# A mixer's transform split into 121 by 25, and its second norm turned by fp8 products

## The reference, cut to what matters

```python
x = conv(x)                      # x: (64, 55, 55, 96); depthwise 25x25, every third tap; gate, bias, residual
t = x.reshape(64, 3025, 96)      # 55 * 55 = 3025 tokens = 25 * 121
# mixer
h = relu(bn1(layernorm(t) @ w1.T))                    # 96 -> 192 channels
X = fft(h, axis=1, norm='ortho')                      # along the 3025 tokens
xr = relu(X.real * diag(r) - X.imag * diag(i) + rb)
xi = relu(X.imag * diag(r) + X.real * diag(i) + ib)
y = ifft(xr + 1j * xi, axis=1, norm='ortho').real
t = t + bn2(y @ w2.T)                                 # 192 -> 96
# feed-forward: inputs and weights of each product rounded to 5 exponent and 2 mantissa bits
n = q8(layernorm(t))
a = relu(q16(q16(n @ q8(W1).T) + q8(b1)))             # 96 -> 384
t = t + q16(q16(q8(a) @ q8(W2).T) + q8(b2))           # 384 -> 96
```

## Time and profile before

| | |
|---|---|
| median of 3 runs | 6499.09 us (6497.29 to 6509.12) |
| the profiled execution | 6508.48 us |
| its span | 6506.7 us |
| mean granted TensorE clock | 0.923 |
| TensorE busy | 5635.0 us (87%) |
| VectorE busy | 4653.9 us (72%) |
| ScalarE busy | 3317.6 us (51%) |
| GpSimd busy | 2185.0 us (34%) |

### The profile page before, as it was taken

How to read it: one execution, slowest core, us unless ns; L and a number is a source line. 1 busy time by engine, 2 the same in 40 slices (tenths; PEclk the granted TensorE clock), 3 DMA queues, 4 the chain that set the end, 5 groups by cost and what they waited for, 6 DMA issues and landing times. The chain is left out here.

```text
span 6506.7 us, 139542 instructions
## 1 busy us (share of the span) xinstructions
PE 5635.0 (87%) x43722; PEld 4751.2 (73%) x43722; DVE 4653.9 (72%) x13238; ACT 3317.6 (51%) x6661; POOL 2185.0 (34%) x1924
## 2 busy tenths in 40 slices
PE   8899994698888888888888888888888888888886
PEld 8898994577777777777777777777777777777775
DVE  4555664367777777777777777777777777777776
ACT  0000000356666666666666666666666666666664
POOL 0000000134444444444444444444444444444443
PEclk9999997789999999999999999999999999999996
DMA  6666664455555555555555555555555555555552
GB/s 219 181 179 189 178 184 113 101 128 132 128 129 129 129 129 128 128 127 128 127 128 128 128 128 128 128 128 128 128 129 129 129 129 128 128 129 129 129 127 60
DMA packets 877318, 875.70 MB, mean 135 GB/s; under 512 B 433439, under 2 KB 805535, under 8 KB 868895
## 3 DMA queue, kind: packets, MB, share of 16 engines
q1 hardware_dynamic: 806005, 784.39, 48.8%
q10 hardware_dynamic: 71174, 89.35, 4.5%
HBM read 497.81 MB, written 375.77 MB: 134 GB/s over the span
## 5 line engine op out<-in xcount | busy, mean ns | idle before, releaser
L646 POOL TENSOR_TENSOR spec<-spec,gc 96x385 f32<-96x385 f32 x512 | 485.7, 949 | 2506.6 <-DVE spec L837 2506.6
L655 POOL TENSOR_TENSOR z<-z,b2q 110x384 f16<-110x384 f16 x448 | 558.7, 1247 | 1622.7 <-ACT z L753 1622.7
L978 PEld LDWEIGHTS ps<-fb,acol 110*96 110x96 f32 (+1 forms) x7168 | 737.9, 164 | 358.9 <-DVE gv L841 230.6
L978 PE MATMUL ps<-fb,acol 110*96 110x110 f32 (+1 forms) x7168 | 817.9, 264 | 122.3 <-DVE gv L841 110.7
L686 ACT ACTIVATE hid<-ps,rstd 110x192 f32<-110x192 f32 x1792 | 660.0, 427 | 487.8 <-PE ps L948 487.2
L958 PE MATMUL ps<-hid,fa 110*110 110x384 f32 x1792 | 754.8, 503 | 165.7 <-ACT hid L686 83.0
L1005 PE MATMUL ps<-w2t,spec 97*110 97x96 f32 x3584 | 742.6, 293 | 13.7 <-DVE spec L848 6.2
L948 PE MATMUL ps<-w1t,xnt 97*110 97x192 f32 x3584 | 734.1, 327 | 0.6 <-ACT xnt L678 0.6
L245 DVE SCALAR_TENSOR_TENSOR xout<-cps,xin 114x351 f32<-114x351 f32 (+3 forms) x512 | 402.4, 786 | 443.4 <-PE cps L272 443.4
L1007 PE MATMUL ps<-w2t,spec 96*110 96x96 f32 x3584 | 718.4, 286 | 0.0
L827 DVE COPY arow<-ps 110x384 f32<-110x384 f32 x896 | 494.6, 552 | 288.0 <-PE ps L958 218.1
(11 more groups left out here) (103 smaller groups left out, 11789.9 us busy)
## 6 DMA issues: line engine op xcount, KB each, us to landing
a_d<-arow SPq DMA_DIRECT2D x896, 165.0 KB
acol<-a_d SPq DMA_DIRECT2D x64, 1155.0 KB
acol<-a_d SPq DMA_DIRECT2D x64, 1113.8 KB
out<-o_sb SPq DMA_DIRECT2D x832, 82.5 KB
xin<-in_x SPq DMA_DIRECT2D x256, 211.5 KB, 5.4
g_d<-mixed SPq DMA_DIRECT2D x64, 660.0 KB
x_d<-xout ACTq DMA_DIRECT2D x144, 263.2 KB
tok<-x_d SPq DMA_DIRECT2D x64, 577.5 KB
```

The source lines that it names most:

```text
L655: nc.gpsimd.tensor_tensor(z16[c % 2][:, :, :], z16[c % 2][:, :, :], b2, ALU.add).then_inc(z_biased, 1)
L978: last = nc.tensor.matmul(ps[0:HH, 2 - 2 * (t % 2) + n // 4, 128 * (n % 4):128 * (n % 4) + NP], acol[0:kk, k1, hf * HH:(hf + 1) * HH], fb[ ...
```

## The change

The transform is split into 121 by 25. A token is u (121) and s (25), 3025 without padding. A tile has 121 partitions and 25 columns; chunks have 4, 4, 4, 4, 3, 3, 3 columns (`CHUNK`), the last three second halves have one. The first half of the transform is over u; of 121 frequencies 61 are kept (`KH`), and two of them share a product with 25 columns each, real and imaginary: 100 partitions (`Q`), 31 pairs (`PAIRS_K`) in place of 28 frequencies. `rows` writes 128 partitions (`M`). The gates' tiles have 8, 8, 8, 7 pairs of 50 elements (400 and 350), `mix` and `inverse` go by 5, 5, 5, 4, 4, 4, 4 pairs (`MIXED`). Tokens, spectra and output need one transfer where two stood. The fills of `tok`, `t_res` and `grow` with zeros go.

Apart from that `xn2` becomes fp8, written so by VectorE, and it is turned by a plain product with an fp8 identity in place of a transpose by the f32 one.

```diff
-K1 = R // 2 + 1
-J = 28
-NP = 2 * R
+U = 121
+S = 25
+N = U * S
+KH = U // 2 + 1
+PAIRS_K = (KH + 1) // 2
+SLOTS = PAIRS_K + 1
+M = 4 * SLOTS
+Q = 4 * S
+CHUNK = (0, 4, 8, 12, 16, 19, 22, 25)
+MIXED = (0, 5, 10, 15, 19, 23, 27, 31)
+GROUP = (0, 8, 16, 24, 31)
+PART = (0, 7, 13, 19, 25)
...
+        ident8 = sb("ident8", [U, U], F8)
...
-        xn2 = sb("xn2", [NP, J, C])
+        xn2 = sb("xn2", [U, S, C], F8)
...
-                nc.vector.memset(tok[:, :, 0:C], 0.0)
-                for v in (t_res, grow):
-                    nc.vector.memset(v[:, :, :], 0.0)
+                nc.vector.memset(mixed[:, PAIRS_K, :], 0.0)
+                nc.vector.tensor_copy(ident8[:, :], ident[0:U, 0:U], saturate=False)
...
-                        for pp in range(2):
-                            sp.dma_start(a_d[i, :, pp * J + JC * c:pp * J + JC * (c + 1), :],
-                                         arow[c % AR][pp * R:(pp + 1) * R, :, :]).then_inc(a_stored[c % AR], 16)
+                        c0, c1 = CHUNK[c], CHUNK[c + 1]
+                        sp.dma_start(a_d[i, c0:c1, :, :].rearrange("s m h -> m s h"),
+                                     arow[c % AR][:, 0:c1 - c0, :]).then_inc(a_stored[c % AR], 16)
...
-                    for ri in range(2):
-                        src = a_d[i, ri * K1:ri * K1 + K1 - ri, 0:R, :].rearrange("k n h -> n k h")
-                        sp.dma_start(acol[ri * R:(ri + 1) * R, ri:K1, :], src).then_inc(acol_in, 16)
+                    src = a_d[i].rearrange("s (r p) h -> (s r) p h", p=SLOTS)
+                    for p0, p1 in ((0, 16), (16, PAIRS_K)):
+                        sp.dma_start(acol[:, p0:p1, :], src[:, p0:p1, :]).then_inc(acol_in, 16)
...
-                    for j in range(JC * c, JC * (c + 1)):
+                    for j in range(CHUNK[c], CHUNK[c + 1]):
                         last = nc.vector.tensor_scalar(xn2[:, j, :], t2[:, j, :], mean2[1][:, j:j + 1],
-                                                       rstd[1][:, j:j + 1], ALU.subtract, ALU.mult)
+                                                       rstd[1][:, j:j + 1], ALU.subtract, ALU.mult, saturate=False)
...
-                    nc.tensor.matmul(ps[0:NP, 7, 0:2 * H], fa[:, :],
-                                     hid[h % 2][:, :, :].rearrange("p j h -> p (j h)"),
+                    n = half(h)[1] - half(h)[0]
+                    nc.tensor.matmul(ps[0:M, 7, 0:n * H], fa[:, :],
+                                     hid[h % 2][:, 0:n, :].rearrange("p j h -> p (j h)"),
...
-                    for n in range(JC):
-                        k1 = c * JC + n
-                        o = ps[0:NP, c % 2, n * C:(n + 1) * C]
-                        nc.tensor.matmul(o, spec[0:HH + 1, 0, k1, :], w2t[0:HH + 1, 0, :],
+                    for p in range(MIXED[c], MIXED[c + 1]):
+                        n = p - MIXED[c]
+                        o = ps[0:Q, c % 2, n * C:(n + 1) * C]
+                        nc.tensor.matmul(o, spec[0:HH + 1, 0, p, :], w2t[0:HH + 1, 0, :],
...
-                        for j in range(JC):
-                            last = nc.tensor.transpose(ps[0:C, 4 + c % 2, 128 * j:128 * j + NP],
-                                                       xn2[:, JC * c + j, :], ident[0:NP, 0:NP])
+                        pe.sem_inc(pe_passed, 1)
+                        for j in range(CHUNK[c + 1] - CHUNK[c]):
+                            last = nc.tensor.matmul(ps[0:C, 4 + c % 2, 128 * j:128 * j + U],
+                                                    xn2[:, CHUNK[c] + j, :], ident8[:, :], start=True, stop=True)
```

More of the change, by code:

```diff
@@ L110, with half @@
 ROOT_C = 3
-QJ = J // 4
-PAIRS = NC * 2
 TILE_AT = (0, 2, 4, 6, 7, 9, 10, 12)
-TOK = JC * NP
+def half(h):
+    c0, c1 = CHUNK[h // 2], CHUNK[h // 2 + 1]
+    return (c0, c0 + 2) if h % 2 == 0 else (c0 + 2, c1)
 def transform_constants():
[L119 to L130, removed]
-    co, si = np.cos(th) / R, np.sin(th) / R
[L132 to L144, removed]
@@ L313, in mixer_stage @@
[L313 to L317, removed]
-        xn2 = sb("xn2", [NP, J, C])
-        xq = sb("xq", [C, J * NP], F8)
+        b2q = sb("b2q", [U, C], F16)
+        tok = sb("tok", [U, S, C + 1])
+        xnt = [sb(f"xnt{s}", [C + 1, JC, U]) for s in range(2)]
+        hid = [sb(f"hid{s}", [U, 2, H]) for s in range(2)]
+        arow = [sb(f"arow{s}", [M, JC, H]) for s in range(AR)]
@@ new lines, in mixer_stage @@
+        acol = sb("acol", [Q, PAIRS_K, H])
+        spec = sb("spec", [HH + 1, 2, PAIRS_K, Q])
+        gc = [sb(f"gc{s}", [HH, KC, Q // 2]) for s in range(2)]
+        gq = [sb(f"gq{s}", [HH, KC, Q // 2]) for s in range(2)]
+        gv = [sb(f"gv{s}", [HH, KC, Q // 2]) for s in range(2)]
+        mixed = sb("mixed", [Q, SLOTS, C])
+        grow = sb("grow", [M, S, C])
+        t_res = sb("t_res", [U, S, C])
+        t2 = sb("t2", [U, S, C])
+        xn2 = sb("xn2", [U, S, C], F8)
+        xq = sb("xq", [C, N], F8)
@@ L331, in mixer_stage @@
+        rstd = [sb(f"rstd{s}", [U, S]) for s in range(2)]
         ps = ctx.enter_context(nc.psum_tensor("ps", [128, 8, 512], F32))
@@ L688, in relu @@
+                    act.wait_ge(a_done, i * HALVES + max(h - 1, 0))
+                    s0, s1 = half(h)
+                    for j in range(s1 - s0):
+                        last = nc.scalar.activation(hid[h % 2][:, j, :], ps[0:U, 5 + h % 2, j * H:(j + 1) * H],
+                                                    ACT.Relu, scale=rstd[0][:, s0 + j:s0 + j + 1])
                     last.then_inc(hid_ready, 1)
                 def gate_in(t):
[L691 removed]
+                    p0, p1, _, hf = group(t)
@@ L709, in part @@
                     turn_out(0)
-                for h in range(PAIRS + 2):
-                    if first and 1 <= h <= PAIRS:
+                for h in range(HALVES + 2):
+                    if first and 1 <= h <= HALVES:
                         relu(h - 1)
@@ L863, in residual_stats @@
                     dve.wait_ge(t2_ready, (i - 2) * NC + c + 1)
-                    return stats(t2, 1, JC * c, JC * (c + 1))
+                    return stats(t2, 1, CHUNK[c], CHUNK[c + 1])
                 if second:
                     dve.wait_ge(w2_done, (i - 1) * NC)
-                for h in range(PAIRS + 3):
-                    if first and 2 <= h < PAIRS + 2:
+                for h in range(HALVES + 3):
+                    if first and 2 <= h < HALVES + 2:
                         rows_out(h - 2)
```

305 lines of the change are left out of this document (164 added, 141 removed).

## The result

| | before | changed |
|---|---|---|
| median | 6498.19 us (4 runs) | 6906.34 us (4 runs, 6899.69 to 6923.9) |
| ratio | | 1.0635 (95%: 1.0609 to 1.0661) |
| span of the profiled execution | 6506.7 us | 6899.0 us |
| mean granted TensorE clock | 0.923 | 0.823 |
| one iteration of the mixer's loop | 81.93 us | 88.74 us |

A forecast was written before the change was run, and what follows sets the result against it. VectorE was taken to bound stage A, TensorE and its clock much of stage C; -3.8 us gave 74.5 at full clock, a fall 78.5; 59 x 3.4 plus ends, -232, gave about 6270 us, range 6020 to 6440.

The forecast's parts named there:

- The work at full clock: One iteration of the mixer's loop without a clock fall: 78.3 us less 3.8, so 74.5 us.
- stage A: First 33.1 us (turns, first products, spectra), bounded by VectorE: fewer copies and norm operations, -1.2 us.
- stage B: Next 6.8 us, where the second norm is turned: shorter turns and evictions, `mix(0)` +0.2; sum -0.4 us.
- stage C, first part: `up(0)` to the second `down`: wider `mix`, `inverse` and `up`, partly covered by less idle time; +0.3 us.
- middle: Chunk steps of stage C with TensorE full: 4.27, 3.94, 3.78, 3.30 us for 4.17 three times and 3.57; -0.8.
- end: Fourth inverse row product to the next first copy, VectorE's and GpSimd's chain: fewer elements and statistics, -1.7 us.
- The clock: One fall an iteration, earlier, in stage B, priced at 3.6 to 5.1 us, taken as 4.0: 78.5 us.
- Slower: Rival, chance 0.10: clock falls in stage B, low until mid stage C (25 us); 84.0 us an iteration, about 6590 us.
- The first rival: Chance 0.17: no clock fall in the steady part; 74.5 us an iteration, about 6025 us.
- Transfers: Loads and stores of spectra, `acol` and `tok`: bytes same within 5%, other run lengths, waits stay hidden.
- The ends: Setup fills -8.4 us, first `acol` wait -5, shorter first and last iterations -16; about -30, bounds 15 and 45.

The follow-up runs named there:

- after_fill: The changed kernel with ten idle products (128x128 f32, into a bank nothing reads) in TensorE's waits of stage B; 6150.81 us, ratio 0.9451.
- before_fill: The kernel before with seven idle products (128x128 f32) ahead of the second `down`; 6295.95 us, ratio 0.9676.
- after_rows128: The changed kernel with `mix` and `up` on 128 rows of the array, the added rows holding zeros; 6261.22 us, ratio 0.9618.
- split_only: The changed kernel with the second norm in f32 and its turn by f32 transposes again, 121 by 25 kept; 6177.81 us, ratio 0.9488.
- best: The changed kernel with `mix` and `up` on 128 rows, six idle products in stage B and eight ahead of the last `down`; 6098.11 us, ratio 0.9366.
- after_fill32: The changed kernel with ten idle products in stage B standing on 32 rows of the array, not 128; 6444.73 us, ratio 0.9899.

## Why the prediction was wrong, by its own steps

**The work at full clock** came out within 0.3 us of the sum in each part but the last. TensorE's rows at the edges of the stages, of the iteration of before without a fall and then of after_fill (first `rows`, last `rows`, `up(0)`, second `down`, fourth `inverse_rows`, first `rows` of the next):

```profile
1443.11 0.85 PE L958 MATMUL ps<-hid,fa 110*110 110x384 f32 x2
...
1477.18 0.90 PE L958 MATMUL ps<-hid,fa 110*110 110x384 f32 x2 [1.32 <-ACT hid L686]
...
1484.64 0.72 PE L1048 MATMUL ps<-xq,w1q 96*128 96x440 fp8e5 x3 [0.80 <-ACT xq L726]
...
1494.10 0.78 PE L1064 MATMUL ps<-w2q,hq 128*110 128x96 fp8e5 x12 [1.81 <-issue]
...
1510.90 0.82 PE L928 MATMUL ps<-grow,ia 110*110 110x384 f32 x2
...
1520.94 0.85 PE L958 MATMUL ps<-hid,fa 110*110 110x384 f32 x2
```
```profile
3010.59 0.83 PE L992 MATMUL ps<-hid,fa 121*128 121x384 f32 x2
...
3043.57 0.59 PE L992 MATMUL ps<-hid,fa 121*128 121x192 f32 x2
...
3050.68 0.77 PE L1092 MATMUL ps<-xq,w1q 96*128 96x484 fp8e5 x3 [0.74 <-ACT xq L750]
...
3060.20 0.84 PE L1108 MATMUL ps<-w2q,hq 128*121 128x96 fp8e5 x12 [1.15 <-issue]
...
3076.30 0.83 PE L961 MATMUL ps<-grow,ia 128*121 128x384 f32 x2
...
3086.14 0.83 PE L992 MATMUL ps<-hid,fa 121*128 121x384 f32 x2
```

| | before | after_fill | measured | forecast |
|---|---|---|---|---|
| stage A | 34.07 | 32.98 | -1.09 | -1.2 |
| stage B | 7.46 | 7.11 | -0.35 | -0.4 |
| stage C, first part | 9.46 | 9.52 | +0.06 | +0.3 |
| middle | 16.80 | 16.10 | -0.70 | -0.8 |
| end | 10.04 | 9.84 | -0.20 | -1.7 |

The end is the one term clearly mis-sized, by 1.5 us. I took `hq`'s cast of 1.33 us as its length and scaled it by elements (-0.23), and the relu with it (-0.1). The relu grew by 0.82 us instead, while the cast shrank by 0.41: together 0.7 of the 1.5. How the rest divides isn't traced. The whole change at full clock is -2.3, not -3.8 (77.83 to 75.55 by these rows; from the 77.6 of before_fill it is -2.0). That the iteration comes out at 75.5 us and not at 76 is luck: the base of 78.3 was 0.5 too long, since I had cut it at the transfers of `t_res`. 75.5 for 74.5 makes 59 us of the error.

**The clock** is the step that failed. "A fall there drags `mix(0)`, `up`, `mix(1)` ... I price it at 3.6 (as now) to 5.1": the place was right (stage B, in the turns), the length was not. I carried 10.2 us over from the kernel before as if it belonged to the fall. It depends on what TensorE runs behind the fall. Before, the low stretch began at the second `down`, with the first `inverse_rows` 6.7 us behind it (3046.70 to 3053.45). Moved to stage B, three chunks of `mix`, `up`, `inverse` lie ahead of it, on 97, 96, 96 and 100 rows (`inverse` had 110 before), at half speed; after_rows128 shows that these rows make the stretch long. The stretch is 30.7 us, with another of 3.4 that the longer idle time before the last `down` brings. Half of 34.1 is 17.1; 88.74 - 75.51 = 13.2 is what shows, the rest lay over waits. That is 9.2 us an iteration over the 4.0 that I took, 543 us of the 636 between forecast and result.

**The rivals.** The third, "Slower", with 0.10, was the one: its mechanism word for word, and 84.0 us where 88.74 was measured, since it had 25 us and no second fall. That the sign hung on the length of one stretch, for which I had a single example, should have given it far more, and the range should have reached past its 6590. The first rival (no fall) describes after_fill and best. Of the rule behind it, the Trainium skill (TensorE: Matmul & The Clock Gate, Part 4: PE-mode transpose) says that transposes don't count for the clock as matmuls do. Here the measurement decides against it: with f32 transposes in stage B the clock held (split_only), with about half as much time of plain fp8 products in their place it fell (the changed kernel). And in before_fill, where it fell at the last `rows`, it rose 3.4 us later, in 24 of 36 cases in the middle of f32 transposes.

**Transfers** were hidden as forecast: after_fill and best move the same bytes in the same runs, at 75.5 us an iteration. VectorE's wait for `tok` grew from 1.58 to 2.76 us (best, at 3038.41), and the idle time behind it that covers it shrank from 1.46 to 0.39. **The ends**: best saves 408.5 us of span, of which 59 iterations of 81.93 - 75.57 are 375, so 33 for the ends where 30 were forecast; in part that is luck, since its idle products and added rows help the last parts too. In the changed kernel 59 x 6.81 = 402 stand beside 392.3 more span, so only 10. Most of the other 20 us went at the end: from the last part's first copy of spectra to the last instruction 233.0 us pass before, 248.4 in the changed kernel and 221.6 in best.

## What to carry to other kernels

Price a fall of the clock by what stands behind it in TensorE's queue, not by the last one seen: look in the traces for the products behind which the clock rose, see how far away they stand from the new place of the fall, and walk there at half speed. Where only one length has been seen, let the range hold one three times as long, as it was here (30.7 for 10.2). Work taken out of a waiting stretch of TensorE can cost more than it saves; f32 transposes or idle products in the wait were cheap cover here. And where a product leaves rows of the array empty, padding them with zeros cost no time here and may bring the clock back sooner: 3.5% in the kernel before, 9.3% (6906.34 to 6261.22) in the changed one.

## What the runs showed of the hardware that was not expected

TensorE's clock does not rise for every busy stretch. Over 20 us without a gap, of products on 96 to 100 rows with `down` on 128 between them, left it at 1.2 GHz; with `mix` and `up` on 128 rows it rose in `mix(1)`. It does not take all 128: in the kernel before it rose at 3056.9, behind `inverse` and `inverse_rows` on 110 rows and a `down`. And 100 are not always too few: in after_fill32 24 stretches of 17 to 24 us ended ahead of any `inverse_rows`. How many rows are enough, beside what else, these runs don't settle. The Trainium skill (TensorE: Matmul & The Clock Gate, Part 1) tells the rise as a matter of sustained activity in time and doesn't speak of rows; this case's low stretch of 30.7 us doesn't fit that.

Three of VectorE's f16 operations on 363 elements took from 0.75 us, with GpSimd idle, to 1.62, with two of GpSimd's operations across them. A duration read from one place of a trace can hold another engine's work in it.
